# One core, three GRU layers and routed experts: normalising moved from VectorE to ScalarE, and an expert stage that ends slot by slot

## Chip, cores and metric

One Trainium2 chip, one core of it. The number that counts is the device time of one execution in microseconds (us), as the median of several runs. TensorE is called PE here, VectorE DVE, ScalarE ACT, GpSimd POOL, SyncE SP, as the profile calls them.

## What is computed

64 graphs of 128 nodes with 128 features. A graph network of three layers (one GRU cell, the same weights in each layer, a message weight for each) runs on the normalised features; its result is added to x. Then a mixture of 8 experts runs on the normalised rows, each of the 8192 rows through the one expert that its gate picks, scaled by that probability, and is added again.

```python
def _gru_cell(inp, h, ...):
    gi = inp @ w_ih.T + b_ih;  gh = h @ w_hh.T + b_hh
    r = sigmoid(i_r + h_r);  z = sigmoid(i_z + h_z);  n = tanh(i_n + r * h_n)
    return (1.0 - z) * n + z * h
for i in range(3):                       # h starts as layernorm(x)
    m = einsum('bnd,de->bne', h, weight[i])
    aggr = einsum('bst,bsd->btd', adj != 0, m)
    h = _gru_cell(aggr, h, ...)
x = x + h
xf = layernorm(x).reshape(-1, 128)
H = gelu(xf @ W1 + b1)                   # 512 hidden
probs = softmax(H @ Wg + bg);  assign = argmax(probs)
out = sum_e where(assign == e, probs[:, e] * (H @ Wd[e] + bd[e]), 0)
x = x + out
```

All of it is float32. Products that need more than one pass are split by the kernel into a high and a low part (`three` issues three matmuls for one product).

## The kernel before

The program is written by hand for each engine: five instruction streams in one block, ordered by semaphores (`wait_ge` before an instruction, `then_inc` on it). Nothing is scheduled by a planner. `hold` is `wait_ge` that leaves out counts of zero.

**Recurrence.** Graphs are taken in groups of 4 (`GR`), so a tile is 128 partitions by 512 columns (`NT`), and groups in batches of 4 (`QUAD`). A unit `u` is one layer of one group; a batch has 12 units in the order of layers: units 0 to 3 are layer 0 of its four groups, 4 to 7 layer 1, 8 to 11 layer 2. There are 4 batches and 48 steps; in step `s` PE works on unit `s`, and the other engines on units near it. Each step has 18 matmuls of 128x512 for the gates, four transposes and eight 128x128 matmuls for the next unit's aggregation. `ahead(s)` says how many units ahead the preparing of a new group is done: from step 3 on, row statistics 9 units ahead (`STATS`), 1/sqrt of the variance 8 ahead (`SCALE`, POOL), the normalising 5 ahead (`NORMAL`), its split into high and low 2 ahead (`SPLIT`, `rows_high` on ACT), the adjacency 2 ahead (`EDGES`). Only units of layer 0 (`first(u)`) have this work, so the normalising falls in steps 7 to 10, 19 to 22 and 31 to 34, and the statistics with their scales in steps 3 to 7, 15 to 19, 27 to 31. The first batch's is done in steps -3 to 2.

In one step, in the order of each engine's stream:

- DVE (`step_gnn`, L787 to L868): low part of the aggregate (L814), new state of unit s-2 (`state`, L793, waits for POOL), residual of finished units (L798), four `bn_stats` of a new group (`row_stats`, L740), normalising of two of its four graphs (`normalise`, L750), some small work (`between`), low part of the next message input (L806 or L803), two candidate operations (L835, L850), `row_moments` (L746), normalising of the other two graphs, adjacency (L809).
- ACT (L644): high part of the aggregate (L648), tanh (L638), high part of the transposed state (L658 or L656), two sigmoids (L663, L665), high part of the state (L672), `rows_high` (L642).
- POOL (L324): two operations on the state of unit s-1 (L336, L338), for a new group the variance plus epsilon (L344) and its power of -0.5 (L346), low part of the state (L352).

**Gate stage** (`gate_step`), 16 groups: PE turns normalised rows, computes the hidden layer (12 matmuls of 128x512), the gate logits and ranks. DVE picks the expert and a position for each row, POOL scatters each graph's 128 rows (with mean, scale, probability and token number) into `sorted_rows` in DRAM (`indirect_dma_start`, L378). The scales of the rows are made by POOL for 16 graphs at once (`row_scales`, L358): batches 0 to 2 during the recurrence, the last in POOL's gate step 8. The row statistics of groups 12 to 15 are taken one by one between the routing operations of DVE's gate steps 2 to 5.

**Expert stage** (`step`): `sorted_rows` is read in slots of 128 rows of one expert; `SLOTS` is 72, in 18 groups of 4 (`SGROUPS`). In step `s` PE computes the hidden layer of group s, turns group s+1, and multiplies group s-1 by its experts' weights (L597; 4 slots of 4 pieces, 32 matmuls as recorded), and signals `e_y` once for the group. DVE then adds the bias for each slot (`product`, L1087), applies probability and residual (`result`, L1091), and POOL scatters each slot to the output (L389). The output banks are `pAG` and `pF`, by turns.

Of the kernel before, what the change touches and what calls it, by code (L numbers as in the profile page):

```python
# [29 lines left out]
P = 128  # L30
# [7 lines left out]
def build(nc, x, adj, W, w_ih, w_hh, b_ih, b_hh, W1, b1, Wg, bg, Wd, bd, out):  # L38
# [12 lines left out]
    SLOTS = -(-((TOK + E * (P - 1)) // P) // GR) * GR  # L51
    SGROUPS = SLOTS // GR
# [11 lines left out]
    with ctx:  # L64
# [38 lines left out]
        mv = sb("mv", [P, QUAD, GR, 2])  # L103

# [61 lines left out]
        bn_ok, mv_ok, var_ok, rstd_ok, xn_ok = (sem(n) for n in ("bn_ok", "mv_ok", "var_ok", "rstd_ok", "xn_ok"))  # L166
# [74 lines left out]
        FFN_LOADS = 16 * 6  # L241
        block = ctx.enter_context(nc.Block())

        @block.sync
        def _(sp):
# [23 lines left out]
            def load_rows(sg):  # L269
                start = [sp.value_load(row_tab[0:1, sg * GR + j:sg * GR + j + 1], min_val=0, max_val=E * REGION)  # L270
                         for j in range(GR)]
                if sg >= RING:
                    sp.wait_ge(e_yo, (sg - RING + 1) * GR)
                for j in range(GR):
                    sp.dma_start(rows[:, sg % RING, j, :], sorted_rows[bass.ds(start[j], P), :]).then_inc(
                        e_in[sg % RING], 16)
# [19 lines left out]
            sp.wait_ge(e_out[0], SLOTS // 2 * 16)  # L296
            sp.wait_ge(e_out[1], SLOTS // 2 * 16)

        @block.gpsimd
        def _(pool):  # L300
# [23 lines left out]
            def step_gnn(s):  # L324
# [57 lines left out]
            def step(s):  # L382
                if inside(s - 1, SGROUPS):
                    b = (s - 1) % 2
                    pool.wait_ge(e_home, s)
                    for j in range(GR):
# [15 lines left out]
        def _(pe):  # L402
# [96 lines left out]
            def hidden(xb, chunks, done):  # L499

                for k in chunks:
                    w = slice(k * P, (k + 1) * P)
                    three(HB[k][:], w1_hi[:, w], w1_lo[:, w], hT_hi[:, xb, :], hT_lo[:, xb, :],
# [62 lines left out]

            def step(s):
                if inside(s, SGROUPS):
                    pe.wait_ge(e_xhi, s + 1)
                    pe.wait_ge(e_xlo, s + 1)  # L570
                    if s == 0:
                        pe.wait_ge(g_h, GROUPS * KC)
                    hold(pe, e_h, s * KC)
                    hidden(s % 2, range(KC), e_w1)
                if inside(s + 1, SGROUPS):
                    b = (s + 1) % 2
                    pe.wait_ge(e_xn, (s + 2) * GR)
                    for j in range(GR):
                        last = nc.tensor.transpose(pT[:, j * P:(j + 1) * P], xn[:, b, j * P:(j + 1) * P], ident[:])
                    last.then_inc(e_t, 1)  # L580
                if inside(s - 1, SGROUPS):

                    b = (s - 1) % 2
                    o = (pAG, pF)[b]
# [7 lines left out]
                    hold(pe, e_yb, (s - 2) * GR)  # L592
                    for j in range(GR):
# [555 lines left out]
```

## Time and profile before

| | |
|---|---|
| median of 3 runs | 616.34 us (614.23 to 619.32) |
| the profiled execution's own time | 614.54 us |
| its span in the trace | 612.8 us, so 1.7 us lie around it |
| busy in the span | PE 526.5 us (86%), DVE 409.4 (67%), POOL 372.4 (61%), ACT 311.2 (51%) |
| recurrence, 0 to about 313 us | PE's granted clock 1.00 from 24 us on |
| gate stage, to about 445 us | PE's clock mostly 0.8 to 1.0 |
| expert stage, to the end | PE's clock mostly 0.7 to 1.0 |

Busy shares of the whole span say little here, because the three stages have different limits. The rows below are read stretch by stretch. In the rows, "idle before" names the engine whose signal came last; "issue" and "remote" are idle times for which the profile shows no releaser.

### The profile page before, as it was taken

What the parts mean: (1) busy time and instruction counts of PE and PEld (TensorE: products, weight loads), DVE (VectorE), ACT (ScalarE), POOL (GpSimd) and SP (SyncE); (2) the same over time, 40 slices, a digit from 0 to 9 for tenths busy, and PEclk for the clock granted to TensorE, in tenths of its full rate; (3) what the DMA queues carried; (4) which work ended last, traced back from release to release, by engine and by line L of the source; (5) the groups of instructions that cost most, each with busy time, mean ns of one, the idle gap of its engine ahead of it and who ended that gap; (6) DMA issues with size and microseconds to landing.
All of it is one profiled execution on the core that took longest, in us unless ns stands there. A gap on an engine that the chain in (4) does not pass through costs nothing.

```text
span 612.8 us, 10175 instructions
## 1 busy us (share of the span) xinstructions
PE 526.5 (86%) x2987; PEld 428.4 (70%) x2987; DVE 409.4 (67%) x1218; ACT 311.2 (51%) x516; POOL 372.4 (61%) x340
## 2 busy tenths in 40 slices
PE   4899899998999989998999779777878797979960
PEld 2778778886788777886776556554767686968960
DVE  4588997899978999799879445543443353454521
ACT  3476557665566655765676546445412333323410
POOL 3289776897598966886744475454445344455552
PEclk9799999999999999999999889799789798988975
DMA  5344460000000000000000111123212222221100
GB/s 141 104 120 123 120 178 2 0 1 0 2 2 1 0 2 1 1 1 1 2 1 19 35 36 36 36 58 88 62 49 73 65 68 62 65 71 42 36 31 0
DMA packets 37363, 26.53 MB, mean 43 GB/s; under 512 B 6060, under 2 KB 33968, under 8 KB 37312
## 3 DMA queue, kind: packets, MB, share of 16 engines
q1 hardware_dynamic: 32160, 17.36, 10.7%
q0 software_dynamic: 4352, 8.53, 4.1%
q8 instruction: 26, 0.43, 0.3%
q14 instruction: 25, 0.20, 0.1%
q10 hardware_dynamic: 800, 0.00, 0.1%
HBM read 16.75 MB, written 9.65 MB: 43 GB/s over the span
## 4 chain that ended last, share of the span: by engine, by line
PE 64%; DVE 19%; issue 5%; ACT 3%; another core or an unknown queue 3%; DMA 1%; DVEq 1%; POOL 1%; SPq 0%; POOLq 0%
PE bank L405 13%; PE bank L407 12%; PE bank L406 12%; PE bank L597 10%; DVE xn L750 5%; PE bank L486 3%; PE bank L485 3%; DVE hT L793 3%; PE bank L527 2%; PE bank L540 2%; PE bank L456 2%; DVE ag_lo L814 2%; DVE cand L835 2%; DVE cand L850 2%
## 5 line engine op out<-in xcount | busy, mean ns | idle before, releaser
L686 ACT ACTIVATE adj_i<-bank,b1c 128x512 f32<-128x512 f32 x136 | 89.7, 687 | 112.7 <-PE bank L407 69.6
L389 POOL DMA_INDIRECT out_dram<-cand,home x72 | 71.0, 986 | 75.9 <-DVE cand L1091 60.1
L378 POOL DMA_INDIRECT sorted_rows<-xrow,pos x64 | 61.9, 967 | 68.2 <-issue 42.8
L336 POOL TENSOR_TENSOR diff<-hT,n_sb 128x512 f32<-128x512 f32 x48 | 77.3, 1610 | 29.7 <-ACT n_sb L638 29.6
L597 PE MATMUL bank<-wd_sb,adj_i 128*128 x576 | 76.2, 290 | 16.1 <-issue 11.2
L597 PEld LDWEIGHTS bank<-wd_sb,adj_i 128*128 128x128 f32 x576 | 72.3, 204 | 18.0 <-issue 17.9
L338 POOL TENSOR_TENSOR diff<-z_sb,diff 128x512 f32<-128x512 f32 x48 | 65.8, 1370 | 3.8
L405 PE MATMUL bank<-hT_hi,w_hi 128*128 128x512 f32 x136 | 63.3, 465 | 5.4 <-DVE hT_lo L1064 2.8
L405 PE MATMUL bank<-ag_hi,wf_hi 128*128 128x512 f32 x144 | 61.1, 424 | 2.4 <-DVE ag_lo L814 2.4
L485 PE MATMUL bank<-A,hn_hi 128*128 128x128 f32 x192 | 44.9, 271 | 18.1 <-DVE hn_lo L806 15.2
L405 PE MATMUL bank<-hT_hi,whh_hi 128*128 128x512 f32 x144 | 60.0, 417 | 0.0
L1087 DVE TENSOR_TENSOR r_sb<-bank,bd_bc 128x128 f32<-128x128 f32 x72 | 20.6, 291 | 57.8 <-issue 37.2
L406 PE MATMUL bank<-hT_lo,w_hi 128*128 128x512 f32 x136 | 58.1, 427 | 0.0
L407 PE MATMUL bank<-hT_hi,whh_lo 128*128 128x512 f32 x144 | 57.9, 402 | 0.0
L406 PE MATMUL bank<-hT_lo,whh_hi 128*128 128x512 f32 x144 | 57.8, 401 | 0.0
L407 PE MATMUL bank<-hT_hi,w_lo 128*128 128x512 f32 x136 | 57.8, 425 | 0.0
L407 PE MATMUL bank<-ag_hi,wf_lo 128*128 128x512 f32 x144 | 57.1, 397 | 0.0
L406 PE MATMUL bank<-ag_lo,wf_hi 128*128 128x512 f32 x144 | 56.8, 394 | 0.0
L485 PEld LDWEIGHTS bank<-A,hn_hi 128*128 128x128 f32 x192 | 37.2, 194 | 26.4 <-issue 25.0
L352 POOL TENSOR_TENSOR hT_lo<-hT,hT_hi 128x512 fp32r<-128x512 f32 x32 | 41.3, 1290 | 17.3 <-ACT hT_hi L672 17.3
L486 PE MATMUL bank<-A,hn_lo 128*128 128x128 f32 x192 | 46.2, 278 | 0.0
L405 PEld LDWEIGHTS bank<-hT_hi,w_hi 128*128 128x128 f32 x136 | 28.4, 209 | 25.3 <-issue 9.5
(164 smaller groups left out, 1187.2 us busy)
## 6 DMA issues: line engine op xcount, KB each, us to landing
adj_i<-sorted_rows SPq DMA_DIRECT2D x72, 66.0 KB
xrow<-in_x_dram SPq DMA_DIRECT2D x16, 256.0 KB, 2.9
adj_i<-in_adj_dram SPq DMA_DIRECT2D x16, 256.0 KB, 3.2
out_dram<-cand,home POOLq DMA_INDIRECT x72
sorted_rows<-xrow,pos POOLq DMA_INDIRECT x64
sorted_rows<-padrow SPq DMA_DIRECT2D x9, 66.0 KB
bd_bc<-in_L_ffn_bd_dram SPq DMA_DIRECT2D x1, 512.0 KB
w1raw<-in_L_ffn_W_dram SPq DMA_DIRECT2D x1, 256.0 KB
```

The costliest lines, as they stand in the source:

```text
L336: nc.gpsimd.tensor_tensor(diff[:, b, :], hT[:, g, :], n_sb[:, b, :], ALU.subtract).then_inc(diff_ok, 1)
L338: nc.gpsimd.tensor_tensor(diff[:, b, :], z_sb[:, g, :], diff[:, b, :], ALU.mult).then_inc(zd_ok, 1)
L352: nc.gpsimd.tensor_tensor(hT_lo[:, g, :], hT[:, g, :], hT_hi[:, g, :].bitcast(fp32), ALU.subtract).then_inc(htlo_ok, 1)
L378: nc.gpsimd.indirect_dma_start(out=sorted_rows, out_offset=bass.IndirectOffsetOnAxis(ap=pos[:, g, j:j + 1], axis=0), in_=xrow[:, g * GR + ...
L389: nc.gpsimd.indirect_dma_start(out=h_out, out_offset=bass.IndirectOffsetOnAxis(ap=home[:, s - 1, j:j + 1], axis=0), in_=yo[:, b, j, :], in ...
L405: nc.tensor.matmul(o, w_hi, x_hi, start=start, stop=False)
L406: nc.tensor.matmul(o, w_hi, x_lo, start=False, stop=False)
L407: return nc.tensor.matmul(o, w_lo, x_hi, start=False, stop=stop)
L485: nc.tensor.matmul(pAG[:, c], hn_hi[:, u % 2, c], A[:, u % QUAD, c], start=True, stop=False)
L486: last = nc.tensor.matmul(pAG[:, c], hn_lo[:, u % 2, c], A[:, u % QUAD, c], start=False, stop=True)
L597: last = nc.tensor.matmul(o[:, j * P:(j + 1) * P], HT[:, b, k, j * P:(j + 1) * P], wd_sb[:, bass.ds(at + k * P, P)], start=(k == 0), stop= ...
L686: nc.scalar.activation(HT[:, hb, k, :], HB[k][:], ACT.Gelu, bias=b1c[:, k:k + 1]).then_inc(done, 1)
```

## The change

1. In the recurrence, from step 3 on, ACT normalises: four activations `Identity(scale*x + bias)` of 128x128 with a scale and a bias column each, placed between the tanh and the wait for the transposed state. DVE's four `normalise` calls for that unit go. The bias, minus mean times scale, is made by POOL (`shift_by`): one more `tensor_scalar` and one more `tensor_tensor` of 128x4 a unit. The first batch is done as before.
2. The statistics of a new group are taken in two halves in one step, and `row_moments` follows a step later.
3. The statistics of groups 12 and 13 are taken in DVE's gate step 0, of group 14 in gate step 1; only group 15's stay between the routing operations, in gate step 2. The last `row_scales` moves from POOL's gate step 8 to gate step 3, ahead of the first scatter.
4. 71 slots in place of 72, the last group with 3. From group 15 (`FINE`) on the expert stage works slot by slot: PE signals `e_y` after each slot, the slots rotate over three banks, DVE does `product` and `result` of a slot in turn, and the experts of group 16 are laced with the hidden layer of group 17 (`last_rows`).

```diff
-    SLOTS = -(-((TOK + E * (P - 1)) // P) // GR) * GR
-    SGROUPS = SLOTS // GR
+    SLOTS = (TOK + E * (P - 1)) // P
+    SGROUPS = -(-SLOTS // GR)
+    FINE = SGROUPS - 3
...
@@ POOL, step_gnn
                     nc.gpsimd.tensor_scalar(var, var, EPS, None, ALU.add).then_inc(var_ok, 1)
+                    if s >= 3:
+                        nc.gpsimd.tensor_scalar(shift_by[:, u % QUAD, :], mv[:, u % QUAD, :, 0], -1.0, None,
+                                                ALU.mult).then_inc(shift_ok, 1)
                     hold(pool, var_ok, made("first", u))
                     nc.gpsimd.tensor_tensor(var, var, half[:, 0:GR], ALU.pow).then_inc(rstd_ok, 1)
+                    if s >= 3:
+                        pool.wait_ge(shift_ok, 2 * (made("first", u) - QUAD) - 1)
+                        pool.wait_ge(rstd_ok, made("first", u))
+                        nc.gpsimd.tensor_tensor(shift_by[:, u % QUAD, :], shift_by[:, u % QUAD, :], var,
+                                                ALU.mult).then_inc(shift_ok, 1)
@@ POOL, gate_step
-                if s == 8:
+                if s == 3:
                     row_scales(QUADS - 1)
@@ PE, expert stage
+            def expert(sg, j, o):
+                at = pe.value_load(wd_tab[0:1, sg * GR + j:sg * GR + j + 1], min_val=0, max_val=(E - 1) * KC * P)
+                for k in range(KC):
+                    last = nc.tensor.matmul(o, HT[:, sg % 2, k, j * P:(j + 1) * P], wd_sb[:, bass.ds(at + k * P, P)],
+                                            start=(k == 0), stop=(k == KC - 1))
+                return last
+            def slot_alone(sg, j):
+                n = sg * GR + j
+                hold(pe, e_yb, n - 2 if n >= FINE * GR + 3 else FINE * GR)
+                expert(sg, j, YB[(n - FINE * GR) % 3][:, 0:P]).then_inc(e_y, 1)
+            YB = (pF, pX, pAG)
+            def last_rows():
+                one, two = SGROUPS - 2, SGROUPS - 1
+                rows_ready(two)
+                slot_alone(one, 0)
+                hidden(two % 2, (0,), e_w1, cols(two))
+                slot_alone(one, 1)
+                hidden(two % 2, (1, 2), e_w1, cols(two))
+                slot_alone(one, 2)
+                hidden(two % 2, (3,), e_w1, cols(two))
+                slot_alone(one, 3)
+                pe.wait_ge(e_h, SGROUPS * KC)
+                for j in range(slots(two)):
+                    slot_alone(two, j)
@@ ACT
+            def normalise(u):
+                act.wait_ge(shift_ok, 2 * (made("first", u) - QUAD))
+                for j in range(GR):
+                    last = nc.scalar.activation(xn[:, u % QUAD, j * P:(j + 1) * P], xres[:, graph0(u) + j, :], ACT.Identity,
+                                                bias=shift_by[:, u % QUAD, j:j + 1], scale=mv[:, u % QUAD, j, 1:2])
+                last.then_inc(xn_ok, 1)
...
+                if s >= 3 and first(s + ahead(s)[NORMAL]):
+                    normalise(s + ahead(s)[NORMAL])
                 if exists(u):
                     hold(act, t_ps, made("all", u))
@@ DVE, step_gnn
                 if s >= 3:
                     if first(measured):
-                        row_stats(measured)
-                    if first(normal):
-                        dve.wait_ge(rstd_ok, made("first", normal))
-                        normalise(normal, 0)
-                        normalise(normal, 1)
+                        row_stats(measured, (0, 1))
+                    if s > 3 and first(measured - 1):
+                        row_moments(measured - 1)
                     between(s)
...
                     if first(measured):
-                        row_moments(measured)
-                    if first(normal):
-                        normalise(normal, 2)
-                        normalise(normal, 3).then_inc(xn_ok, 1)
+                        row_stats(measured, (2, 3))
@@ DVE, gate_step
-                measured = s - 2 + EARLY_STATS
-                stat = s >= 2 and inside(measured, GROUPS)
+                measured = GROUPS - 1
+                stat = s == 2
+                if s == 0:
+                    gate_measured(GROUPS - 4)
+                    gate_measured(GROUPS - 3)
+                if s == 1:
+                    gate_measured(GROUPS - 2)
@@ DVE, expert stage
+                    if fine:
+                        for j in range(slots(s - 1)):
+                            n = (s - 1) * GR + j
+                            dve.wait_ge(e_y, n + 1)
+                            product(j, YB[(n - FINE * GR) % 3][:, 0:P])
+                            result(j)
+                            if j == 0 and inside(s + 1, SGROUPS):
+                                split_rows(s + 1)
+                    else:
+                        dve.wait_ge(e_y, s * GR)
...
```

## Rows read from the trace of the kernel before

**Rows 1.** Windows, three four-step stretches with normalising; sum (length, then busy us).
```profile
134.27:161.55 27.28, 23.07 (x121) 18.36 (x121) 26.86 (x59) 14.80 (x24) 19.85 (x16) 1.00 0.00 1
...
sum 80.82, PE 69.28 PEld 55.09 DVE 79.25 ACT 44.42 POOL 59.73; mean PE 23.09 PEld 18.36 DVE 26.41 ACT 14.81 POOL 19.91
```
**Rows 2.** Windows, three steps before a stretch: PE, PEld, DVE, ACT, POOL, clock.
```profile
117.67:134.27 16.60, 16.60 (x91) 14.02 (x91) 14.84 (x47) 11.12 (x19) 15.86 (x15) 1.00 0.00 1
```
**Rows 3.** Groups by form: what goes, and relatives of what comes (busy, mean ns).
```profile
L750 DVE SCALAR_TENSOR_TENSOR xn<-xrow,mv 128x128 f32<-128x128 f32 x64 | 39.1, 655 | 1.3 <-POOL mv L346 1.3
...
L663 ACT ACTIVATE r_sb<-bank,bsum 128x512 f32<-128x512 f32 x48 | 33.1, 690 | 4.7
...
L648 ACT ACTIVATE ag_hi<-bank 128x512 fp32r<-128x512 f32 x48 | 28.7, 598 | 31.8 <-PE bank L486 31.8
...
L754 DVE BATCH_NORM_STATS2 gstats<-xrow 128x6 f32<-128x128 f32 x64 | 15.8, 279 | 0.0
...
L642 ACT ACTIVATE hn_hi<-xn 128x512 fp32r<-128x512 f32 x16 | 10.0, 627 | 0.8 <-DVE bsum L782 0.8
...
L759 DVE BATCH_NORM_AGGREGATE xrow<-gstats 128x2 f32<-128x6 f32 x64 | 5.9, 153 | 0.0
...
L707 ACT ACTIVATE th<-sh 128x32 f32<-128x32 f32 x16 | 3.6, 223 | 3.8 <-DVE sh L924 3.8
...
L663 ACT ACT_TABLE_LOAD x1 | 1.3, 1283 | 0.0
```
**Rows 4.** Timeline, one PE-bound step (start, length, engine and line, idle before).
```profile
56.94 0.71 ACT L638 ACTIVATE n_sb<-cand,bi 128x512 f32<-128x512 f32 x1
...
59.02 0.60 ACT L658 ACTIVATE hn_hi<-bank 128x512 fp32r<-128x512 f32 x1 [1.38 <-PE bank L456]
...
59.66 0.69 DVE L806 TENSOR_TENSOR hn_lo<-bank,hn_hi 128x512 fp32r<-128x512 f32 x1 [0.26 <-ACT hn_hi L658]
...
60.92 0.22 PE L485 MATMUL bank<-A,hn_hi 128*128 128x128 f32 x1
```
**Rows 5.** Timeline of POOL, one step in which it makes scales.
```profile
130.32 1.74 POOL L336 TENSOR_TENSOR diff<-hT,n_sb 128x512 f32<-128x512 f32 x1
132.14 1.30 POOL L338 TENSOR_TENSOR diff<-z_sb,diff 128x512 f32<-128x512 f32 x1
133.41 0.23 POOL L344 TENSOR_SCALAR mv<-mv 128x4 f32<-128x4 f32 x1
133.72 1.04 POOL L346 TENSOR_TENSOR mv<-mv,half 128x4 f32<-128x4 f32 x1
...
135.99 1.74 POOL L336 TENSOR_TENSOR diff<-hT,n_sb 128x512 f32<-128x512 f32 x1
```
**Rows 6.** Timeline of DVE, the operation that takes POOL's result of Rows 5.
```profile
135.50 1.07 DVE L793 TENSOR_TENSOR hT<-n_sb,diff 128x512 f32<-128x512 f32 x1
```
**Rows 7.** Timeline of DVE, first gate step.
```profile
316.60 0.69 DVE L775 TENSOR_TENSOR hT_lo<-bank,hT_hi 128x512 fp32r<-128x512 f32 x1 [2.05 <-ACT hT_hi L681]
```
**Rows 8.** Timeline of PE, the same place.
```profile
317.44 0.63 PE L494 MATMUL bank<-ident,xn 128*128 128x128 f32 x4 [0.25 <-DVE hT_lo L775]
```
**Rows 9.** Timeline of POOL: the last power and the scatter after it.
```profile
363.37 2.96 POOL L364 TENSOR_TENSOR xrow<-xrow,half 128x16 f32<-128x16 f32 x1
367.70 1.11 POOL L378 DMA_INDIRECT sorted_rows<-xrow,pos  x1 [1.38 <-DVE pos L945]
```
**Rows 10.** Timeline of PE, expert products of groups 15 and 17.
```profile
575.40 3.74 PE L597 MATMUL bank<-wd_sb,adj_i 128*128 x32
...
590.00 6.58 PE L597 MATMUL bank<-wd_sb,adj_i 128*128 x32 [1.11 <-ACT adj_i L686]
```
**Rows 11.** Windows, from the start of the last hidden layer to PE's end.
```profile
578.90:596.59 17.69, 13.98 (x79) 12.57 (x77) 4.66 (x18) 2.75 (x4) 10.36 (x11) 0.81 0.11 35
```
**Rows 12.** Timeline of POOL, first and last of the last group's four scatters.
```profile
599.50 0.98 POOL L389 DMA_INDIRECT out_dram<-cand,home  x1 [2.85 <-DVE cand L1091]
...
603.36 0.98 POOL L389 DMA_INDIRECT out_dram<-cand,home  x1 [0.30 <-issue]
```

More of the change, by code:

```diff
@@ L241, in build, with slots, cols, sent @@
         FFN_LOADS = 16 * 6
+        def slots(sg):
+            return min(GR, SLOTS - sg * GR)
+        def cols(sg):
+            return slots(sg) * P
+        def sent(half):
+            return sum(slots(sg) for sg in range(SGROUPS) if sg % 2 == half)
         block = ctx.enter_context(nc.Block())
@@ L618, in _ @@
             table(2)
-            for s in range(3, SGROUPS + 1):
+            for s in range(3, SGROUPS - 1):
                 step(s)
+            last_rows()
         @block.scalar
@@ L681, in turned_high, with gelus @@
                 nc.scalar.activation(hT_hi[:, g % 2, :], pT[:], ACT.Copy).then_inc(g_xhi, 1)
-            def gelus(hb, s, chunks, ready, done):
+            def gelus(hb, s, chunks, ready, done, n=NT):
                 for k in chunks:
                     hold(act, ready, s * KC + k + 1)
-                    nc.scalar.activation(HT[:, hb, k, :], HB[k][:], ACT.Gelu, bias=b1c[:, k:k + 1]).then_inc(done, 1)
+                    nc.scalar.activation(HT[:, hb, k, 0:n], HB[k][:, 0:n], ACT.Gelu, bias=b1c[:, k:k + 1]).then_inc(done, 1)
             HB = (pR, pZ, pGH, pGI)
@@ L734, in _, with row_stats @@
             dve.wait_ge(c_gp, 8)
-            def row_stats(u):
+            def row_stats(u, part):
                 dve.wait_ge(data_in, (group(u) + 1) * 32)
-                for j in range(GR):
+                for j in part:
                     last = nc.vector.bn_stats(stats[:, u % QUAD, j, :], xres[:, graph0(u) + j, :])
-                last.then_inc(bn_ok, 1)
+                if part[-1] == GR - 1:
+                    last.then_inc(bn_ok, 1)
             def row_moments(u):
@@ L754, in gate_stats, with gate_measured @@
                 return nc.vector.bn_stats(gstats[:, g % 2, j, :], xres[:, g * GR + j, :])
+            def gate_measured(g):
+                dve.wait_ge(x1_ok, g + 1)
+                for j in range(GR):
+                    last = gate_stats(g, j)
+                last.then_inc(g_bn, 1)
+                gate_moments(g)
             def gate_moments(g):
@@ L1059, in rest, with split_rows @@
                 ts(tab[:, 0:1], rsum[:], first_used[:, 0:1], float(E * REGION), ALU.add, ALU.min).then_inc(t_made, 1)
+            def split_rows(sg):
+                n = cols(sg)
+                dve.wait_ge(e_xhi, sg + 1)
+                tt(hT_lo[:, sg % 2, 0:n], pT[:, 0:n], hT_hi[:, sg % 2, 0:n].bitcast(fp32), ALU.subtract).then_inc(e_xlo, 1)
             def step(s):
[L1062 to L1064 removed]
+                fine = s - 1 >= FINE
+                if inside(s + 1, SGROUPS) and not fine:
+                    split_rows(s + 1)
                 if inside(s + 2, SGROUPS):
                     b, r = (s + 2) % 2, (s + 2) % RING
[L1067 removed]
+                    dve.wait_ge(e_in[r], landed(s + 2, RING) - (GR - slots(s + 2)) * 16)
                     hold(dve, e_t, s + 1)
[L1069 removed]
+                    for j in range(slots(s + 2)):
                         ts(xn[:, b, j * P:(j + 1) * P], rows[:, r, j, 0:P], rows[:, r, j, MEAN:MEAN + 1],
@@ L1092, in result @@
                             ALU.mult, ALU.add).then_inc(e_yo, 1)
-                    product(0)
-                    for j in range(1, GR):
-                        product(j)
-                        result(j - 1)
-                    result(GR - 1)
+                    if fine:
+                        for j in range(slots(s - 1)):
+                            n = (s - 1) * GR + j
[3 more added lines that the diff above has]
+                            if j == 0 and inside(s + 1, SGROUPS):
+                                split_rows(s + 1)
+                    else:
+                        dve.wait_ge(e_y, s * GR)
+                        product(0, o[:, 0:P])
+                        for j in range(1, GR):
+                            product(j, o[:, j * P:(j + 1) * P])
+                            result(j - 1)
+                        result(GR - 1)
+            YB = (pF, pX, pAG)
             for s in range(-3, UN):
```

76 lines of the change are left out of this document (36 added, 40 removed).

## The prediction, made before the changed kernel was run

> **What bounds the kernel now.** I read the clock and busy time by windows first, because the shares of the whole span mix three stages. In three recurrence steps without normalising PE is busy 16.60 of 16.60 us at clock 1.00 [rows 2]: 5.53 us a step, and nothing but fewer matmuls could shorten them. In the twelve steps with normalising PE is busy 69.28 of 80.82 us and DVE 79.25 [rows 1]: DVE is the limit there. The groups by form say why: a 128x128 normalising operation on DVE takes 655 ns in the mean [rows 3], and four of them stand in such a step, two of them ahead of the low part of the message input that PE waits for. At the end of the program the timeline and windows show a second weak place: from the last hidden layer on PE needs 17.69 us of which it is busy 13.98, at clock 0.81 [rows 11], and after PE's end at 596.58 us [rows 10] the last scatter starts only at 603.36 [rows 12].
>
> **Normalising on ACT: the gain.** The twelve steps take 80.82 us [rows 1]. At PE's own pace they would take 12 x 5.53 = 66.4 [rows 2]. The gain is at most 14.4 us; it cannot be more, as PE is then full. It is reached if the next-latest engine stays within 5.53 us, so ACT and POOL must be looked at.
>
> ACT gets four activations of 128x128 from SBUF. A 128x512 copy from SBUF takes 627 ns and a 128x32 one 223 [rows 3], so a column costs 0.84 ns and 128 columns about 304 ns. A bias column adds about 92 ns (690 against 598 [rows 3]). A scale column is in no row: between nothing and another 92 ns. So one costs 0.40 to 0.49 us and four 1.6 to 2.0; I take 1.8, since a column of scales is read as a column of biases is. They start when the tanh ends, 56.94 + 0.71 = 57.65, in a gap of 1.38 us in which ACT waits for PE's transposes [rows 4]. So the copy at 59.02 moves back by 0.2 to 0.6. Behind it DVE's low part ends at 59.66 + 0.69 = 60.35 and PE takes it at 60.92: 0.57 us of cover [rows 4]. Cost 0 to 0.03 a step. ACT's total is 3.71 us a step (11.12 / 3 [rows 2]), 5.5 with the new work: it just fits, and the upper price would cost 0.2 a step. I book 0.3 us for all twelve steps, range 0 to 2.4. If the cover of 0.57 were gone, it would be up to 12 x 0.6 = 7.
>
> The Trainium skill ("ScalarE: Activation LUTs", What ACT_TABLE_LOAD costs) gives 186 ns + 0.833 ns a column, 93 ns for each pointer operand and an overlap of 93 ns between neighbours. By that figure the four would take an estimated 1.64 us, the low end of my bracket, and the sum would be 0.3 us lower. The fixed part and the bias column agree with the rows above; the scale column is its word alone.
>
> **The shift, on POOL.** Each of the twelve units adds a 128x4 `tensor_scalar` and a 128x4 product that waits for the power. The nearest row for the first is 0.23; for the second the same shape costs 0.23 as an addition and 1.04 as a power [rows 5]. I take 0.25, as the power function is the only reason for 1.04 on four columns, so +0.55 with the wait between, range 0.4 to 1.4. POOL has no room in these steps: it starts a unit every 135.99 - 130.32 = 5.67 us [rows 5], already over PE's 5.53. With 6.2 it falls back 0.7 a step. Its result, ready at 132.14 + 1.30 = 133.44 [rows 5], is taken by DVE at 135.50 [rows 6]: 2.06 us of slack in the third of the four steps. Two additions are made before it, so about 0.96 is left there, 0.3 in the fourth and -0.4 in the step after. DVE can start its state 1 us later before the next operation misses ACT's copy, and PE has the 0.57 behind that. Then POOL has only about (19.85 - 1.27) / 4 = 4.6 us of work a step [rows 1, 5] and catches up. Cost 0. At the upper price it falls back 1.5 a step, DVE starts the state 0.6 late in the third step already and some 3.6 late at the end; after the 1.5 of cover that is about 2.1 us in each of three batches, 6.3 in all.
>
> **Statistics in halves.** The same instructions in other places, in steps where DVE is busy 14.84 of 16.60 [rows 2]. The moments come a step later, still well before POOL's scale. Cost and gain 0, bounds -0.5 and +0.5.
>
> **Gate stage.** Groups 12 and 13's statistics now stand ahead of the low part for which PE waits. One group's cost (15.8 + 5.9) / 16 = 1.36 us of DVE time [rows 3], so 2.7 for two. DVE is idle for 2.05 before that low part [rows 7], and PE waits for it at once [rows 8]: +0.65 at most, I take 0.45 because neighbours overlap. Group 14's 1.36 stands ahead of the next low part; most of it meets slack that the first delay leaves. Together +0.6, bounds 0 and 1.7. In gate steps 3 to 5 DVE's routing gets shorter by the same amount, but PE fills its time there, so nothing comes back. The moved power frees POOL from 363.37 to 366.33, but the scatter behind it waits 1.38 us for its positions [rows 9]: it was hidden, gain 0. In its new place it waits for group 15's statistics and holds the first scatter; nothing downstream needs that scatter soon. 0, bounds 0 and +1.
>
> **End of the expert stage.** A group's products take 578.90 - 575.40 = 3.50 us at full clock and 6.58 for the last group, after a wait of 1.11 for ACT [rows 10, 11]. One slot fewer and a quarter of a hidden layer fewer are 0.9 + 0.7 = 1.6 us of PE time. The lacing puts a slot of group 16 over the wait for the last activation: 1.1. The slow clock costs 3.08 on four slots; three slots and a shorter idle before them keep two thirds of it: 1.0 gained, bounds 0 and 3.1. Tail: before, the last scatter starts 603.36 - 596.58 = 6.8 us after PE's end and the first 2.9 [rows 12], because the four start together and each takes 1.29. Slot by slot the last scatter starts as the first does now, about 2.9 after PE's end: 3.9 gained, bounds 3.0 and 4.5. Against it, PE enters group 15's products only when DVE has finished all of group 14: 0.4, bounds 0 and 1. Together -7.2, bounds -4 and -10.
>
> **Sum.** -14.4 + 0.3 + 0 + 0.6 - 7.2 = -20.7. From the profiled execution, 614.5 to 593.8; taken from the median of the runs, 1.8 us higher, 616.3 to 595.6.
>
> **Rivals.**
> - *The recurrence keeps part of its length.* POOL at its upper price is the mechanism (the product costs as the power, 1.04): +6.3, so 602. For it: POOL is busy 15.86 of 16.60 us just where the work is added [rows 2]. Against it: 0.23 for the addition. ACT at its upper price without cover ends at about the same time. 15%.
> - *Unexplained stops.* PE and ACT stop at times for which no releaser is shown; of the 3.7 us that PE is idle at the end, only 1.11 is a wait for ACT [rows 10, 11]. They can fall elsewhere in the changed streams. If another such stop hits the laced end or the gate stage, 4 to 5 us are lost: 600. If one goes, 591. 10% each. The Trainium skill ("Runtime: NRT & Kernel Launch", Instruction fetch mechanics) says that fetching instructions in blocks is mostly hidden; by that rule the stops would have another cause and stay where they are, and the time would be my forecast.
> - *Slower: ACT changes its tables.* If Identity is not in the table set in which sigmoid and tanh are, each such step has two table loads of 1.28 us [rows 3]. Then ACT adds 1.8 + 2.6 - 1.38 - 0.57 = 2.4 us to a step, 29 in all against 14.4 gained: 616.3 + 29 - 14.4 - 6.6 = 624. The kernel is slower from (14.4 + 6.6) / 12 = 1.75 us of delay a step on. Against it: copies run between the sigmoids without a load, and the trace has three loads in all. 2%. The Trainium skill ("ScalarE: Activation LUTs", Table sets) states that identity and copy are in every set, which speaks against this rival.
>
> **How the numbers follow.** The forecast has 63%, 595.6 us, with its own range 592 to 600; the rivals 15, 20 and 2%. From 590 to 604 both stops and the kept recurrence are inside, and about 2 in 10 is left out. A measurement of this kernel can tell about 1%, 6 us, from no change: under 610 has 96%, within 1% 2%, slower 2%.
>
> **What will show it.** Steps 7 to 10 of each batch at 5.5 to 5.6 us and PE full in them; the four activations 0.40 to 0.49 us each; POOL's new product near 0.25; POOL without idle for about five steps a batch, and DVE's state starting closer to its result. At the gate's start PE waits some 0.5 us longer for DVE. The last scatter starts about 3 us after PE's end. The prediction is wrong if the steps stay over 5.8, if table loads appear, or if the end gains less than 4.

## The result

The changed kernel takes 593.73 us (median, 590.85 to 596.25); the kernel before, run beside it, took 615.94 (614.23 to 619.32). The ratio is 0.9635, 95% interval 0.9587 to 0.9683: 22.2 us faster. The forecast was 595.6. The profiled execution of after is 592.61 us, its span 590.9 against 612.8. Ratios and their intervals are of fast executions alone, the medians below of all: beside the others one of kernel 4 took 829.0 us, one of kernel 10 713.5, and one of the kernel before, beside kernel 12, 1444.39.

The windows of the three four-step stretches with normalising (length, then the busy time of PE, PE's loads, DVE, ACT, POOL, then the granted clock, as in [rows 1]):
```profile
61.85:83.98 22.13, 22.13 (x121) 18.68 (x121) 15.24 (x28) 20.52 (x40) 20.11 (x22) 1.00 0.67 183
129.99:152.13 22.14, 22.14 (x121) 18.70 (x121) 18.00 (x48) 20.53 (x41) 20.55 (x22) 1.00 0.00 1
198.14:220.27 22.13, 22.13 (x121) 18.68 (x121) 18.00 (x48) 20.52 (x40) 20.54 (x22) 1.00 0.00 1
sum 66.40, PE 66.40 PEld 56.06 DVE 51.23 ACT 61.57 POOL 61.19; mean PE 22.13 PEld 18.69 DVE 17.08 ACT 20.52 POOL 20.40
```
The twelve steps take 66.40 us where they took 80.82 [rows 1], and PE is busy in all of it. This is the forecast's 12 x 5.53, and it has nothing left to give. DVE fell from 79.25 to 51.23; ACT and POOL are now both over 90% busy there.

The new work by groups, and ACT's timeline in such a step (compare [rows 3, 4]):
```profile
L699 ACT ACTIVATE xn<-xrow,shift_by,mv 128x128 f32<-128x128 f32 x48 | 19.7, 483 | 0.0
...
L363 POOL TENSOR_TENSOR mv<-mv,half 128x4 f32<-128x4 f32 x12 | 13.5, 1121 | 0.0
...
L367 POOL TENSOR_TENSOR shift_by<-shift_by,mv 128x4 f32<-128x4 f32 x12 | 3.6, 303 | 1.7
...
L360 POOL TENSOR_SCALAR shift_by<-mv 128x4 f32<-128x4 f32 x12 | 2.7, 228 | 0.9
```
```profile
131.10 1.64 ACT L699 ACTIVATE xn<-xrow,shift_by,mv 128x128 f32<-128x128 f32 x4
132.64 0.59 ACT L723 ACTIVATE hn_hi<-bank 128x512 fp32r<-128x512 f32 x1
...
133.26 0.69 DVE L880 TENSOR_TENSOR hn_lo<-bank,hn_hi 128x512 fp32r<-128x512 f32 x1 [0.73 <-ACT hn_hi L723]
```
An activation with both columns lasts 483 ns and four in a row 1.64 us. They fill the 1.38 us that ACT had before the turned rows, so the next copy starts without a gap, some 0.1 us later in its step than in [rows 4], and DVE's low part still meets PE. POOL's product takes 0.20 us in the median and 0.30 in the mean (the longest, 0.64), not the power's 1.04.

POOL, two consecutive steps (to be read with [rows 5]):
```profile
121.08 1.74 POOL L350 TENSOR_TENSOR diff<-hT,n_sb 128x512 f32<-128x512 f32 x1
...
124.79 1.04 POOL L363 TENSOR_TENSOR mv<-mv,half 128x4 f32<-128x4 f32 x1
125.97 0.53 POOL L367 TENSOR_TENSOR shift_by<-shift_by,mv 128x4 f32<-128x4 f32 x1
126.46 1.29 POOL L374 TENSOR_TENSOR hT_lo<-hT,hT_hi 128x512 fp32r<-128x512 f32 x1
127.71 1.30 POOL L350 TENSOR_TENSOR diff<-hT,n_sb 128x512 f32<-128x512 f32 x1
129.09 1.29 POOL L352 TENSOR_TENSOR diff<-z_sb,diff 128x512 f32<-128x512 f32 x1
...
133.56 1.29 POOL L350 TENSOR_TENSOR diff<-hT,n_sb 128x512 f32<-128x512 f32 x1
...
141.25 1.30 POOL L352 TENSOR_TENSOR diff<-z_sb,diff 128x512 f32<-128x512 f32 x1
```
```profile
142.59 1.76 DVE L867 TENSOR_TENSOR hT<-n_sb,diff 128x512 f32<-128x512 f32 x1 [0.20 <-POOL diff L352]
```
No gap at all, and the steps start 6.63 and 5.85 us apart: it falls back 0.7 us a step on PE's 5.53, as the forecast says. DVE takes the result of 129.09 + 1.29 = 130.38 at 131.30, 0.92 us later. Two steps on nothing is left of that: DVE waits 0.20 us for POOL at 142.59, and again in the third batch, in the first it has 0.3 us to spare. No step gets longer by it.

The gate's first steps (compare [rows 7, 8]; there the waits were 0.25 and none):
```profile
303.04 0.63 PE L516 MATMUL bank<-ident,xn 128*128 128x128 f32 x4 [0.44 <-DVE hT_lo L849]
...
309.25 0.63 PE L516 MATMUL bank<-ident,xn 128*128 128x128 f32 x4 [0.31 <-DVE hT_lo L849]
```
The end, PE and then POOL (compare [rows 10, 12]):
```profile
560.92 6.37 PE L603 MATMUL bank<-wd_sb,adj_i 128*128 x40 [2.34 <-DVE r_sb L1165]
568.68 1.15 PE L603 MATMUL bank<-wd_sb,adj_i 128*128 x8 [0.87 <-DVE r_sb L1165]
...
573.70 2.31 PE L603 MATMUL bank<-wd_sb,adj_i 128*128 x16 [0.51 <-issue]
576.83 1.15 PE L603 MATMUL bank<-wd_sb,adj_i 128*128 x8 [0.81 <-DVE r_sb L1165]
```
```profile
577.30 0.98 POOL L411 DMA_INDIRECT out_dram<-cand,home  x1 [1.75 <-DVE home L1161]
...
581.48 0.98 POOL L411 DMA_INDIRECT out_dram<-cand,home  x1 [0.30 <-issue]
```
The last scatter starts 581.48 - 577.98 = 3.5 us after PE's end, before it was 6.8. But PE now waits for DVE three times: 2.34 us where it enters group 15's products, which need all of group 14 done by DVE (the forecast had 0.4 for this, at most 1), and then 0.87 and 0.81 us for DVE to empty one of the three banks.

Where the 21.9 us of span are: 14.7 in the recurrence (266.55 us against 281.23, from the start of the second to that of the last of ACT's 48 copies of the aggregate's high part), -0.7 given back at the gate's start, 4.3 from the last group's high part to the end of the span (31.8 against 36.1). The other 3.6 lie between, where both kernels have stops with no releaser; the experiments deal with them.

### The profile page after: what moved, and what is told of

It is laid out like the page before. It is cut to its first block, busy times and chain, and to the rows that moved or that the text cites. A ratio compares the mean times of both kernels' runs of the same rounds, so it can differ in the third digit from the quotient of the medians.

```text
span 590.9 us, 10170 instructions
## 1 busy us (share of the span) xinstructions
PE 519.7 (88%) x2978; PEld 423.8 (72%) x2978; DVE 381.4 (65%) x1167; ACT 326.9 (55%) x564; POOL 374.9 (63%) x363
## 4 chain that ended last, share of the span: by engine, by line
PE 68%; DVE 10%; another core or an unknown queue 8%; ACT 6%; issue 4%; DMA 1%; DVEq 1%; SPq 0%; POOL 0%; POOLq 0%; ACTq 0%
PE bank L427 15%; PE bank L429 14%; PE bank L428 14%; PE bank L603 7%; ACT adj_i L751 4%; PE bank L508 4%; PE bank L507 3%; PE bank L478 3%; PE bank L562 2%; DVE xn L838 2%; PE bank L549 2%; DMA adj_i<-in_adj_dram 1%; PE bank L516 1%; DVE xn L1149 1%
## 5 line engine op out<-in xcount | busy, mean ns | idle before, releaser
L751 ACT ACTIVATE adj_i<-bank,b1c 128x512 f32<-128x512 f32 (+1 forms) x136 | 88.8, 686 | 115.5 <-PE bank L429 73.7
L603 PE MATMUL bank<-wd_sb,adj_i 128*128 x568 | 73.3, 286 | 14.9 <-issue 7.0
L350 POOL TENSOR_TENSOR diff<-hT,n_sb 128x512 f32<-128x512 f32 x48 | 76.4, 1591 | 15.5 <-ACT n_sb L694 15.5
L603 PEld LDWEIGHTS bank<-wd_sb,adj_i 128*128 128x128 f32 x568 | 69.6, 200 | 17.7 <-issue 17.6
L427 PE MATMUL bank<-hT_hi,w_hi 128*128 128x512 f32 (+1 forms) x136 | 62.1, 457 | 6.0 <-DVE hT_lo L1138 3.8
L352 POOL TENSOR_TENSOR diff<-z_sb,diff 128x512 f32<-128x512 f32 x48 | 63.5, 1324 | 3.8
L428 PE MATMUL bank<-hT_lo,w_hi 128*128 128x512 f32 (+1 forms) x136 | 57.3, 421 | 0.3 <-issue 0.3
L429 PE MATMUL bank<-hT_hi,w_lo 128*128 128x512 f32 (+1 forms) x136 | 57.1, 420 | 0.3 <-issue 0.3
L427 PEld LDWEIGHTS bank<-hT_hi,w_hi 128*128 128x128 f32 x136 | 27.7, 204 | 26.3 <-issue 9.2
```

Of the source, the lines that this page charges most:

```text
L350: nc.gpsimd.tensor_tensor(diff[:, b, :], hT[:, g, :], n_sb[:, b, :], ALU.subtract).then_inc(diff_ok, 1)
L352: nc.gpsimd.tensor_tensor(diff[:, b, :], z_sb[:, g, :], diff[:, b, :], ALU.mult).then_inc(zd_ok, 1)
L427: nc.tensor.matmul(o, w_hi, x_hi, start=start, stop=False)
L428: nc.tensor.matmul(o, w_hi, x_lo, start=False, stop=False)
L429: return nc.tensor.matmul(o, w_lo, x_hi, start=False, stop=stop)
L603: last = nc.tensor.matmul(o, HT[:, sg % 2, k, j * P:(j + 1) * P], wd_sb[:, bass.ds(at + k * P, P)], start=(k == 0), stop=(k == KC - 1))
```

## The experiments

Twelve kernels in four sessions. The first four ran on a chip on which the kernel before takes 553.53 us (552.07 to 554.92), 62 us less than in the session of the result; the others on chips like the first, where it took 611.5 to 612.8. Ratios are each against the kernel before on the same chip. I use two lengths beside the times: R, the recurrence from ACT's second to its last copy of the aggregate's high part (before 281.23, after 266.55), and E, from the last group's high part to the end of the span (before 36.1, after 31.8). R is steady to 0.1 us from session to session. E is not: the same program has 31.8 and 32.9, and the old end 36.1 in the session of the result and 31.1 on the faster chip.

**1. The recurrence alone.** The normalising on ACT, the shift on POOL, the statistics in halves; gate and expert stage as before.

> Recurrence part alone (normalising on ACT, statistics in halves), the rest as before. My theory: this is two thirds of the gain; 14.6 us less than before in the recurrence, so a ratio near 0.976, and no step with normalising over 5.6 us. Rival (the end does the most, the recurrence gain is partly given back later in the gate stage): less than 10 us in all.

538.31 us (537.87 to 538.98), ratio 0.9726 (0.9699 to 0.9752): -15.2 us. R = 266.58. The mechanism holds on a chip of other speed to the tenth of a microsecond.

**2. The gate alone.** The early power and the four groups' statistics ahead.
```
-                if s == 8:
+                if s == 3:
                     row_scales(QUADS - 1)
...
+                if s == 0:
+                    gate_measured(GROUPS - 4)
+                    gate_measured(GROUPS - 3)
+                if s == 1:
+                    gate_measured(GROUPS - 2)
```

> Gate part alone (statistics of groups 12 to 14 early, last power ahead of all scatters). My theory: PE waits 0.5 to 0.8 us longer for the low parts of groups 1 and 2, the power was hidden before; +0.7 us, ratio 1.001, not to be told from 1. Rival (the power held up the scatters in the middle of the stage, so that its going pays): 3 us less, 0.995.

554.72 us, ratio 1.0023 (1.0006 to 1.0039): +1.2. Here the steps of the gate are 5.40 us long from the fourth on (one is 6.24, in kernel 3 too), so the cost can be read: against kernel 3, whose gate is the old one, the turned rows' high parts start 0.08 us later at first, 0.19 at the third and 0.79 from the fourth on to the last. So 0.7 us is lost at the second step's low part, and never given back.

**3. The end alone.** 71 slots, the last three groups laced and scattered slot by slot.

> Expert-stage part alone (71 slots and slot by slot). My theory: 7 us less, ratio 0.988, most of it behind the last product of PE, where the last scatter starts 3 to 3.5 us after it and not 6.8. Rival (the gain is the slot that is gone): no more than 3 us, as in the next kernel.

550.13 us, ratio 0.9940 (0.9921 to 0.9959): -3.4, half of what the forecast gave this part.

**4. 71 slots only.** Kernel 3 without the laced part: the last group has three slots, and its hidden layer 384 columns.
```
-    FINE = SGROUPS - 3
+    FINE = SGROUPS
...
-            for s in range(3, SGROUPS - 1):
-                step(s)
-            last_rows()
+            for s in range(3, SGROUPS + 1):
+                step(s)
```

> 71 slots alone: the last group has 3 slots, but signals once for the group and nothing is laced. One slot of products (0.9 us, 1.6 at the slow clock), a quarter of the last hidden layer (0.7), and one scatter of 1.29 us less at the tail: about 3 us less by my theory, ratio 0.995; slot by slot is worth the other 4. Rival: as much as the kernel with all of the end.

551.42 us, ratio 0.9963 (0.9950 to 0.9977): -2.1. The lacing and the scattering slot by slot are worth 1.3 us (E: 31.1 in kernel 2, 28.9 here, 27.7 in kernel 3). The timelines of POOL show why. Kernel 2, whose end is the old one; 4; 3:
```profile
534.05 0.98 POOL L389 DMA_INDIRECT out_dram<-cand,home  x1 [1.52 <-DVE cand L1103]
535.34 0.98 POOL L389 DMA_INDIRECT out_dram<-cand,home  x1 [0.30 <-DVE cand L1103]
...
543.07 0.98 POOL L389 DMA_INDIRECT out_dram<-cand,home  x1 [0.30 <-issue]
```
```profile
531.42 0.98 POOL L401 DMA_INDIRECT out_dram<-cand,home  x1 [0.81 <-DVE cand L1141]
...
539.14 0.98 POOL L401 DMA_INDIRECT out_dram<-cand,home  x1 [0.30 <-issue]
```
```profile
519.73 0.98 POOL L401 DMA_INDIRECT out_dram<-cand,home  x1 [2.07 <-DVE cand L1142]
521.01 0.98 POOL L401 DMA_INDIRECT out_dram<-cand,home  x1 [0.30 <-DVE cand L1142]
...
537.09 1.05 POOL L401 DMA_INDIRECT out_dram<-cand,home  x1 [0.30 <-issue]
538.45 0.98 POOL L401 DMA_INDIRECT out_dram<-cand,home  x1 [0.30 <-issue]
```
A scatter occupies POOL's queue for 1.29 us (534.05 to 535.34). Kernel 2 has eight of them back to back at its end, 4 has seven, and 3 has fifteen between 519.73 and 538.45, only 0.7 us of that being more than 14 x 1.29. On this chip PE does its last products without a wait:
```profile
527.40 7.53 PE L597 MATMUL bank<-wd_sb,adj_i 128*128 x64
```
That is kernel 2; it ends at 534.93, and 8.1 us of scatters follow. Kernel 3's PE ends later, at 535.86, and only 2.6 us follow. With POOL's queue as the limit, PE's saved work and clock are worth nothing; what counts is one scatter fewer and an earlier start of the queue. This is so on this chip, and in kernel 6, which also has eight back to back. In the session of the result the queue was not alone: ahead of the last four scatters POOL is idle for 2.85 us in before [rows 12] and 1.75 in after, both times for DVE.

**5. After itself, in a later session.**

> The whole change, in the session in which its parts were run. Parts add up (my theory): recurrence -15.2, gate +1.2, end -3.4, together -17.4 us, ratio about 0.969. The rival is that the parts lean on each other (the gate with the statistics in halves meets a later or an earlier POOL, the end the other chain of stops): then it is off that sum by more than 2 us, and the -21 to -22 us of the first session would be more than the sum of the parts.

595.55 us (589.89 to 599.07), ratio 0.9747 (0.9686 to 0.9808): -17.3 by the medians, -15.5 by the ratio, whose interval is -11.8 to -19.2. The parts add up to -17.4; R is again 266.55, E 32.9. This ran on another chip than the parts, one on which before takes 612.83 us, so the sum lies in the interval and no more is shown: that the medians agree to 0.1 us is chance. On the chip of the parts the whole change wasn't run. The first session's -22.2 (interval -19.5 to -25.4) is larger than the sum by some 5 us.

**6. VectorE normalises with one tensor operand.** The recurrence of before with
```
-                return stt(xn[...], xres[:, graph0(u) + j, :], mv[:, u % QUAD, j, 0:1],
-                           mv[:, u % QUAD, j, 1:2].to_broadcast([P, P]), ALU.subtract, ALU.mult)
+                return ts(xn[...], xres[:, graph0(u) + j, :], mv[:, u % QUAD, j, 0:1],
+                          mv[:, u % QUAD, j, 1:2], ALU.subtract, ALU.mult)
```

> The recurrence of before, normalising still on VectorE, but with both statistics as scalar columns instead of the scale as a second tensor operand. The prediction takes the loss of the 12 normalising steps as VectorE's amount of work. Theory A: what is dear is the form, a 128x128 instruction that reads two tensors beside POOL; with one tensor it takes 0.25 to 0.35 us instead of 0.5 to 1.3, the 12 steps fall to 5.5 to 5.7 us, and the gain is 11 to 15 us (ratio 0.974 to 0.980). Theory B: the work as such is too much for VectorE in these steps, whatever the form: they stay above 6.1 us and the gain is under 8 us (ratio over 0.985).

611.44 us, ratio 0.9983 (0.9943 to 1.0024); R = 280.27, 1.0 us shorter. Theory A has fallen. For the source line the trace gives the least, the median and the longest duration, in before and in this kernel:
```profile
L750 DVE SCALAR_TENSOR_TENSOR xn<-xrow,mv x64: 337/344/1447, 10.2 to 235.2; 128x128 f32<-128x128 f32 x64
```
```profile
L750 DVE TENSOR_SCALAR xn<-xrow,mv x64: 332/340/1451, 10.6 to 233.3; 128x128 f32<-128x128 f32 x64
```
In both kernels 44 of the 64 take under 0.4 us and 18 take 1.3 to 1.45, with one tensor operand as with two: little more than one POOL operation of 1.29. What the 18 wait for shows beside POOL's timeline (before):
```profile
136.50 2.75 DVE L750 SCALAR_TENSOR_TENSOR xn<-xrow,mv 128x128 f32<-128x128 f32 x2
```
```profile
135.99 1.74 POOL L336 TENSOR_TENSOR diff<-hT,n_sb 128x512 f32<-128x512 f32 x1
137.81 1.29 POOL L338 TENSOR_TENSOR diff<-z_sb,diff 128x512 f32<-128x512 f32 x1
```
The two here last 1.38 and 1.45 us and end 0.15 us after POOL's two operations end (137.73 and 139.10). So do all 18, in kernel 6 0.08 us after. The 655 ns of [rows 3] are a mean over free ones and blocked ones, and nothing about the instruction. So theory B's numbers came, but what fills VectorE in these steps is less the amount of work than the waiting for POOL: free, the four would take 4 x 0.34 = 1.4 us. This agrees with the Trainium skill ("SBUF — State Buffer", Who interferes with whom): by it both a VectorE instruction with two SBUF inputs and a `tensor_scalar` in a two-port mode wait for a GpSimd instruction that holds the shared port, and ScalarE never does. A form with neither was not tried.

**7. One more power on POOL in each of the twelve steps.**
```
+                        nc.gpsimd.tensor_tensor(spare[:, u % QUAD, :], var, half[:, 0:GR], ALU.pow)
```

> After, with one more 128x4 power on POOL in each of the 12 steps that take a power (its result is not used), about 1.1 us of POOL each. POOL has been without a gap in the first steps of each batch. My prediction priced POOL's shift of 0.55 us at nothing because 1.5 us of slack covers what falls behind. If that sum is right, 4 x 1.1 us exceed the slack by about 2.9 us in each of three batches: +6 to +9 us over after. Rival: POOL is not near the bound, its work is taken up by the lag of the low parts: under +1 us. Second rival: POOL is the bound already and each microsecond counts: +13 us.

604.97 us, ratio 0.9886 (0.9822 to 0.9950), 9.4 us over after in the medians; R = 278.33, +11.8. The three batches lose 4.2, 4.4 and 3.2 us for 4 x 0.98 us of added POOL time each. The loss comes in two steps per batch, in which DVE waits 2.0 and then 2.75 us for POOL (here the second):
```profile
149.27 1.74 DVE L869 TENSOR_TENSOR hT<-n_sb,diff 128x512 f32<-128x512 f32 x1 [2.75 <-POOL diff L353]
```
Part of it is the clock. The longer of the two steps, in the second and in the third batch:
```profile
145.19:154.06 8.87, 7.31 (x31) 6.03 (x32) 4.96 (x9) 5.24 (x10) 8.46 (x8) 0.81 0.01 3
217.64:225.37 7.73, 6.00 (x31) 4.85 (x32) 4.63 (x8) 5.25 (x10) 7.57 (x7) 1.00 0.01 2
```
After PE's wait it is granted 0.81 of its clock in the second batch (and in the first), and the same 31 matmuls take 7.31 us; in the third it keeps 1.00 and they take 6.00. So POOL's 3.9 us cost 3.2 a batch, 0.8 is covered, and the clock's fall adds 1.1 to 1.2 in two batches of three. That 11.8 us are lost for 11.8 added is chance. Neither sum is right as it stands: the cover is there, though smaller than the 1.5 of mine, and the clock was in none of them. After loses no time to POOL, but stands on the edge: of what POOL gets there in addition four fifths are paid.

**8. The gate's normalising with one tensor operand.** The edit of kernel 6 in `gate_normal` of after.

> After, with the gate's normalising on VectorE in the form that has one tensor operand and two scalar columns (64 instructions). Theory A of the form: the four of a group fall from up to 3.2 us beside POOL to about 1.1, which lets the low parts of the first gate groups and the last steps of the recurrence come earlier: -2 to -5 us against after. Theory B: the amount of work decides and the form is nothing: within 0.5 us of after.

592.50 us (588.82 to 595.02), ratio 0.9683 (0.9610 to 0.9757); span 588.6 against 588.1 of kernel 5, R = 266.29. The form gives 0.07 us in each of the three long steps. Theory B, as in 6; the medians' 3 us are no gain that the trace shows.

**9. The gate's first three groups normalised on ScalarE.**
```
+                if s - FFN_WEIGHTS in (3, 4, 6):
+                    g = (3, 4, 6).index(s - FFN_WEIGHTS)
+                    act.wait_ge(g_sft, 2)
+                    for j in range(GR):
+                        at = g * GR + j
+                        last = nc.scalar.activation(xn[:, g, j * P:(j + 1) * P], xres[:, at, :], ACT.Identity,
+                                                    bias=g_shift[:, at:at + 1], scale=xrow[:, at, RSTD:PROB])
+                    last.then_inc(g_xn, 1)
...
-                if w in (3, 4, 6):
-                    gate_rows((3, 4, 6).index(w))
```

> After, with the gate's first three groups normalised on ScalarE too (twelve activations with two scalar columns in steps 42, 43 and 45 of the recurrence; POOL makes the 16 shift columns once, two instructions, in a step in which it has gaps). These three steps took 6.97 us where their neighbours take 5.53; VectorE has no gap in them and its four instructions 3.0 to 3.3 us. If VectorE's amount of work is what bounds such a step, as in the 12 normalising steps, all three fall to 5.5 us: -4.3 us against after. Rival: after the relief POOL or the batch of low parts takes the place of VectorE: the steps stay above 6.2 us and the gain is under 2.5 us.

592.94 us (589.12 to 594.09), ratio 0.9711 (0.9644 to 0.9779). One of the three steps, by windows, in kernel 5 and here:
```profile
258.93:265.91 6.98, 5.77 (x31) 4.59 (x31) 6.66 (x12) 3.70 (x7) 5.38 (x4) 1.00 0.00 0
```
```profile
260.08:265.62 5.54, 5.54 (x31) 4.68 (x31) 3.82 (x9) 5.13 (x11) 4.37 (x4) 1.00 0.00 0
```
All three fall to 5.5 us and R to 262.23: -4.3 us, as expected. The whole time shows 2.6 us at most. By the traces' clocks, which start the recurrence 1.2 us apart, the turned rows' high part of this kernel is 3.17 us ahead of kernel 5's when the gate starts and still after four steps, and 3.15 us behind it where the expert stage opens: the gain is lost inside the gate.

**10. After without the changes to the gate.**

> The changes to the recurrence and to the expert stage, without those to the gate (the last power stays where it was, the statistics of the last groups one by one). The gate part alone gave +1.2 us. If this price is a real one and stands beside the faster recurrence too, this kernel is 1 to 1.5 us faster than after. If the price was that of the old recurrence (POOL's backlog at its end), it is within 0.5 us of after or slower.

595.44 us, ratio 0.9757 (0.9687 to 0.9828), not to be told from kernel 5. The 0.7 us are there (from the first to the fourth high part of the gate it gains 0.71 on kernel 5), but from there to the end of the gate it loses 8.2. By groups, PE's wait for ACT's copy of the gate's logits between 300 and 410 us, in kernel 5 and in this one:
```profile
L562 PE MATMUL bank<-pick,lgT 128*128 128x8 f32 x120 | 16.6, 265 | 13.4 <-ACT lgT L767 13.4
```
```profile
L562 PE MATMUL bank<-pick,lgT 128*128 128x8 f32 x112 | 17.0, 279 | 19.1 <-ACT lgT L767 19.1
```
and on the chip of kernels 1 to 4 (kernel 3) this wait is not there at all, only the one for DVE's tables:
```profile
L552 PE MATMUL bank<-pick,lgT 128*128 128x8 f32 x128 | 15.3, 246 | 1.9 <-DVE sh L971 1.9
```
ACT's copy is late because ACT itself stops for 2 to 5 us with no releaser that the trace knows (kernel 5):
```profile
390.85 0.69 ACT L767 ACTIVATE lgT<-bank,bg_col 128x512 f32<-128x512 f32 x1 [5.02 <-remote]
```
Kernels 5, 9 and 10 have six to eight such stops of more than 2 us on ACT in the gate, at other places in each, while kernels 5 and 8, which differ in one instruction's form, have the same seven at the same instructions. They are not tied to the fetching of instructions as far as the trace records it: the packets of its instruction queues take 0.3 to 1.5 us in kernel 3 as in kernel 5, and none lies in the stop of 5.02 us or in five others of kernel 5's seven. PE's clock falls with the stops: it is granted 0.93 from 304 to 380 us in kernel 5, 0.87 in kernel 10, and 1.00 in kernel 3.

**11. Six instead of four activations a step.**
```
+                for j in range(2):
+                    nc.scalar.activation(spare[:, u % QUAD, j, :], xres[:, graph0(u) + j, :], ACT.Identity,
+                                         bias=shift_by[:, u % QUAD, j:j + 1], scale=mv[:, u % QUAD, j, 1:2])
```

> After, with six instead of four activations of this kind in each of the 12 normalising steps (the two more go to a tile that nobody reads). ScalarE's instructions of such a step follow each other in about 5.15 us, of 5.53; two more at about 0.41 us each make 5.97 us. If ScalarE is that near to being the bound, the 12 steps take about 5.97 us: +5 us over after. Rival: the order of its queue spoils more than the sum, since the turned rows' high part stands behind them: +0.82 a step, +10 us. Second rival: the gaps take it all, under +1 us.

592.60 us (590.48 to 596.64), ratio 0.9723 (0.9628 to 0.9819). R = 272.08: +5.5 us, 5.99 us a step, as reckoned (5.97), so neither rival holds. Windows of the first such stretch: ACT 22.67 of 23.95 busy.
```profile
61.58:85.53 23.95, 23.08 (x121) 18.36 (x121) 13.83 (x27) 22.67 (x48) 20.18 (x22) 1.00 0.64 173
```
Yet the whole time isn't longer: by the traces' clocks it is 7.1 us behind kernel 5 at the gate's start, 2.7 at its end and 2.9 at the last group. What 9 and 10 show as a loss works here as a gain.

**12. The best of the parts.** Recurrence, end, and the edit of kernel 9, with the old gate.

> What the runs point to: the changes to the recurrence and to the expert stage, without those to the gate, and with the gate's first three groups normalised on ScalarE. From the step times: -14.6 us in the 12 normalising steps, -4.3 us in steps 42, 43 and 45, the gate's +0.7 us not paid, and -3.4 us at the end as measured alone: -22.3 us, ratio about 0.964 against before, and the start of step 47's record 18.9 us earlier than in before, against 14.6 us in after. Rival: what is saved ahead of the gate is given back to its stops of 2 to 5 us, which stand at other places in every kernel: then the step times show the 18.9 us and the whole time is within 1% of after.

593.33 us (587.06 to 597.53), ratio 0.9750 (0.9677 to 0.9824). R = 262.22, 4.3 us under after and 19.0 under before, and the old gate's 0.7 us show too: the lead over kernel 5 is 5.1 us after four gate steps. It is 2.7 where the expert stage opens and 2.9 at the last group; span 585.3 against 588.1. The rival was right: no version is measurably better than after on these chips. On the chip of kernels 1 to 4 it wasn't run.

## Why the prediction was right, point by point

- *Normalising on ACT, -14.4.* Right, and shown alone by kernel 1: 66.40 us for the twelve steps, -14.4 by the windows. R shows 0.25 us more, from the first steps of the kernel.
- *ACT's cost, +0.3 booked.* No loss can be read; the four take 1.64 us and not 1.8. By the Trainium skill ("ScalarE: Activation LUTs", What ACT_TABLE_LOAD costs) 1.64 was the estimate. The trace agrees: one takes 483 ns where that section's figures, with 93 ns for the scale column, give 479. Kernel 11 shows that ACT's order fits with 0.38 us to spare a step.
- *The shift at nothing.* The outcome was right, and the duration (0.20 in the median, 0.30 in the mean). The slack ran out nearly as forecast: 0.92, 0.54 and 0.03 us in the second batch against 0.96, 0.3 and -0.4. What was too large is the cover of 1.5 us behind it. By kernel 7's third batch, in which 3.9 us more of POOL cost 3.2, it is an estimated 1 us: 0.8 that took up added work, and the 0.2 that DVE already waits in after. Nor had the sum a term for the clock, which falls after such a wait and made 2.3 of kernel 7's 11.8 us. At the upper price of the product, 0.8 us more in each step, the loss would by the same measure be 3 x (4 x 0.8 - 0.8) = 7 us (an estimate), close to the 6.3 of the first rival, if the clock holds.
- *Statistics in halves, 0; moved power, 0.* Right. The power now lies at 312.92 to 315.87, and the first scatter after it held nobody up: in kernel 2 nothing is lost behind the fourth high part.
- *Gate, +0.6.* Right: 0.7 by the high parts; PE's two waits, 0.44 and 0.31, are 0.5 us more than before. Kernels 2, 10 and 12 show it each.
- *End of the expert stage, -7.2.* Too large: -3.4 alone, of which 2.1 for 71 slots. On the slower chips E is 33.6 and 36.1 in the two kernels with the old end and 31.8 to 34.1 in the eight with the new one, 1.8 apart in the mean. Three terms failed. The 1.6 us of PE's work, the 1.1 of lacing and the 1.0 of clock were added to the 3.9 of the tail as if PE set the end; where no stop delays PE, POOL's queue of 1.29 us a scatter sets it, and PE's time is under it. And the wait of 1.11 and the clock of 0.81 in [rows 10, 11] were read as properties of the old end, though without the stops they aren't there: kernel 2 has neither. And the entry to group 15's products, 0.4 in the sum, cost PE 2.34 us in after and 2.1 to 2.8 in kernels 5, 8 and 12.
- *Unexplained stops.* The rival was right in kind. Some 3.6 us of the first session's difference lie where they stand, and this hid the end's missing 3.8. The parts alone give -17.4 and so 598.5, inside the range; the median fell 1.9 us from the forecast because an error and a chance met. By the Trainium skill ("Runtime: NRT & Kernel Launch", Instruction fetch mechanics) the fetching of instructions is mostly hidden; the traces agree as far as they go, since six of kernel 5's seven stops have no packet of the instruction queues in them. Whether fetching has a part in the stops in another way no run here shows.
- *ACT table loads.* None came: after has three in all, as before had.

Still open is what the stops are and why one chip has none. Kernels 9 to 12 show that what is won before the gate starts is not what is won at its end: kernels 9, 10 and 12 lose 2 to 8 us in between against kernel 5, kernel 11 gains 4.

## What to carry to other kernels

A long mean of a short VectorE instruction beside a busy POOL can mean that it is blocked: look at least, median and longest, and at whether the long ones end with a POOL operation. Here another form gained 0.08 us a step, the move to ScalarE 1.2. When you load an engine up to its edge, ask what PE's wait would cost in clock too. Before you price the end of a program, count what the last queue must still issue: where this queue outlasts an engine, as in kernels 2 to 4, work saved on the engine is worth nothing. And where the trace has stops without a releaser, judge an edit by the length of its own stage, and expect of the whole time only its mean over sessions.

## What was not expected of the hardware

- The same program took 553.5 us on one chip and 611 to 616 on others. The recurrence has the same length on both to 0.1 us (281.19 in kernel 2 against 281.23); all but some 2 us of the difference is in the gate, whose later steps take 5.40 us on the one and 4.4 to 13.1 on the others, and in the expert stage, with the stops and the clock that falls after them.
- POOL's power costs 1.04 us on 4 columns and 2.95 on 16, while a product or an addition on 4 columns costs 0.20 to 0.23 in the median.
- A scatter of 128 rows takes 0.98 us of POOL, but they follow each other only every 1.29 us.
